# A four-stage attention and FFN kernel on Trainium2: the hidden units of the expert stage are split before they are transposed, and the order of four engines around it is rewritten

## What is computed

```python
router_logits = x2d @ gate_kernel                      # 2048 x 32
routing_weights, selected_experts = jax.lax.top_k(jax.nn.softmax(router_logits, axis=-1), 8)
routing_weights = routing_weights / jnp.sum(routing_weights, axis=-1, keepdims=True)
w0 = jax.lax.ragged_dot(sorted_inputs, gate_proj, group_sizes)    # 512 -> 192
w1 = jax.lax.ragged_dot(sorted_inputs, up_proj, group_sizes)      # 512 -> 192
inter = jax.nn.silu(w0) * w1
expert_out = jax.lax.ragged_dot(inter, down_proj, group_sizes)    # 192 -> 512
output = jnp.einsum('BKE,BK->BE', per_token, routing_weights)
```

## Time and profile before

| | |
|---|---|
| median of three runs | 1451.62 us |
| profiled execution, first to last instruction (span) | 1474.3 us |
| mean granted TensorE clock in it | 0.977 of full speed |
| PE busy, matmuls | 1382.7 us, 94% |
| DVE, ACT, POOL busy | 1022.1, 505.4, 383.7 us |
| expert stage, first hidden transposition to the last | 871.8 to 1461.9 us |

### The profile page before, as it was taken

The page is one execution under the profiler, slowest core; times in us unless marked ns, Lnnn a source line. Parts: engine busy times, 40 slices in busy tenths (PEclk is TensorE's granted clock), DMA queues, the critical chain, the costliest instruction groups (busy, mean ns, idle before and its releaser), DMA issues.

```text
span 1474.3 us, 26984 instructions
## 1 busy us (share of the span) xinstructions
PE 1382.7 (94%) x7525; PEld 753.2 (51%) x7526; DVE 1022.1 (69%) x2467; ACT 505.4 (34%) x916; POOL 383.7 (26%) x313
## 2 busy tenths in 40 slices
PE   4799999999999999999999559999999999999997
PEld 3344444444444444455444236666666666666664
DVE  7879857976895656688776536666666666666664
ACT  1454543444435343422222113333333333333332
POOL 1000000000000000025556543444344344344443
PEclk9899999999999999999999769999999999999999
DMA  9975776766767778836748668889999888989785
GB/s 370 396 262 193 263 256 213 247 197 205 241 209 237 235 254 286 280 119 251 284 195 294 242 227 216 223 218 260 246 246 234 221 229 228 247 223 222 148 162 84
DMA packets 132696, 345.04 MB, mean 234 GB/s; under 512 B 15008, under 2 KB 19616, under 8 KB 125728
## 3 DMA queue, kind: packets, MB, share of 16 engines
q1 hardware_dynamic: 73488, 206.72, 41.6%
q0 software_dynamic: 34640, 85.74, 25.2%
q10 hardware_dynamic: 24512, 51.89, 10.8%
HBM read 192.68 MB, written 151.62 MB: 234 GB/s over the span
## 4 chain that ended last, share of the span: by engine, by line
PE 68%; DVE 16%; DMA 4%; issue 4%; ACT 3%; another core or an unknown queue 2%; ACTq 1%; SPq 1%; DVEq 0%; POOLq 0%
PE PS L1671 17%; PE PS L1673 17%; PE PS L1672 17%; PE PS L1933 5%; PE PS L1961 2%; PE PS L1962 2%; DMA split_experts<-HT 2%; DMA CST<-in_kv 1%; PE PS L1950 1%; DVE EX L1300 1%; PE PS L1951 1%; DVE EX L1306 1%; DVE nw L1027 1%; DMA X<-in_x 1%
## 5 line engine op out<-in xcount | busy, mean ns | idle before, releaser
L587 POOL DMA_INDIRECT out<-BIG,EX x159 | 247.2, 1555 | 354.9 <-issue 153.4
L1671 PE MATMUL PS<-BIG 128*128 (+1 forms) x795 | 269.5, 339 | 5.0 <-DVE BIG L1572 3.3
L1672 PE MATMUL PS<-BIG 128*128 (+1 forms) x795 | 269.5, 339 | 0.0
L1673 PE MATMUL PS<-BIG 128*128 (+1 forms) x795 | 269.5, 339 | 0.0
L1671 PE MATMUL PS<-HT,BIG 128*128 128x512 f16 (+1 forms) x512 | 194.1, 379 | 3.0 <-DVE HT L1101 1.4
L1672 PE MATMUL PS<-HT,BIG 128*128 128x512 f16 (+1 forms) x512 | 194.0, 379 | 0.0
L1673 PE MATMUL PS<-HT,BIG 128*128 128x512 f16 (+1 forms) x512 | 194.0, 379 | 0.0
L560 POOL DMA_INDIRECT rows_by_expert<-HT,POS x128 | 124.9, 976 | 122.6 <-DVE POS L1391 88.1
L1672 PE MATMUL PS<-BIG,EX 128*128 128x512 f16 (+1 forms) x376 | 143.8, 382 | 1.1 <-issue 1.1
L824 ACT ACTIVATE BIG<-PS 128x256 f16<-128x256 f32 x159 | 61.1, 384 | 243.3 <-PE PS L1951 229.0
L1673 PE MATMUL PS<-BIG,EX 128*128 128x512 f16 (+1 forms) x376 | 143.6, 382 | 0.4 <-issue 0.4
(11 more groups left out here) (264 smaller groups left out, 2218.0 us busy)
## 6 DMA issues: line engine op xcount, KB each, us to landing
BIG<-rows_by_expert ACTq DMA_DIRECT2D x159, 280.0 KB
HT<-in_experts SPq DMA_DIRECT2D x64, 640.0 KB, 4.6
BIG<-split_experts SPq DMA_DIRECT2D x32, 1152.0 KB
split_experts<-HT SPq DMA_DIRECT2D x96, 320.0 KB, 2.2
CST<-in_kv SPq DMA_DIRECT2D x64, 256.0 KB, 4.7
split_context<-RT SPq DMA_DIRECT2D x64, 256.0 KB, 4.5
BIG<-split_context SPq DMA_DIRECT2D x7, 2048.0 KB
rows_by_expert<-X SPq DMA_DIRECT2D x32, 280.0 KB
```

The costliest lines, as they stand in the source:

```text
L587: pool.indirect_dma_start(a_out, bass.IndirectOffsetOnAxis(ap=IDY[:, u % V:u % V + 1], axis=0), yt[u % V], None, compute_op=ALU.add).then_ ...
L1671: mm(out, lh, rh, start=first, stop=False)
L1672: mm(out, lh, rl, start=False, stop=False)
L1673: return mm(out, ll, rh, start=False, stop=last_group)
```

## The change

- **Hidden units.** They are split where they lie, by tokens: ACT rounds to fp16 (`hidden_hi`, 192 columns), DVE subtracts (`hidden_lo`, two pieces of 64 and 128 columns). The four pieces are laid in a row: high 0 to 127, high 128 to 191 beside low 128 to 191, low 0 to 127. PE transposes these three 128 by 128 blocks in fp16 into a PSUM tile of fp16, and ACT copies the 384 columns to SBUF (`hidden_copy`).
- **Down weights.** The second block of 64 rows is now stacked high over high and low over low, so `tile_down` still has five matmuls; an expert takes 2 EW = 5120 columns, 1280 KB, and `split_half` is two equal instructions on DVE in place of three.
- **Order.** In pass t PE runs: transposition of t+3, up of t+2, hidden transposition of t+1, down of t. ACT, DVE follow; LEAD is 7.
- **Registers.** In the loop ACT loads 8 rows and 12 due counts in place of 12 and 16; the counts go through a maximum (`load_counts`), on POOL too. `CH` is one element longer, so all tables lie four bytes further on.
- **First tiles.** ACT issues the gathers 1 to 3, then `tile_silu(0)`, `tile_hi(1)`, the gather of 4 and so on. Two tables that ACT needs first are made and announced first; a further small matmul (PS bank 6) serves them. POOL writes column 4 of token tile 13 ahead of tiles 14 and 15. SP stores the empty rows of eight experts before the loop, not of four.

```diff
-E16 = EW + EL
+E16 = 2 * EW
-LEAD = 6
+LEAD = 7
+LATE = 1
+def load_counts(eng, name, table, least, most):
+    loaded = [eng.alloc_register(f"{name}{i}") for i in range(table.shape[-1])]
+    held = [eng.alloc_register(f"{name}_held{i}") for i in range(table.shape[-1])]
+    eng.reg_load(loaded, table)
+    for to, of in zip(held, loaded):
+        eng.reg_alu(to, of, least, ALU.max)
...
-        CH = ex(1, F16)
+        CH = ex(2, F16)
...
-            for e in range(WP):
+            for e in range(2 * WP):
                 pad_expert(e, 16 * e)
...
-            for t in range(NT - 3, NT):
+            scatter_rows(NT - 3, range(5))
+            for t in range(NT - 2, NT):
                 scatter_rows(t, range(4))
...
             def hidden_hi(t, p):
-                act.wait_ge(s_at, t + 1)
-                act.activation(eah[p], PS[:, 4, 0:2 * P], ACT.Copy).then_inc(s_ah2, 1)
+                act.wait_ge(s_ea, t + 1)
+                act.activation(es[p][:, 0:M], ea[p], ACT.Copy).then_inc(s_ah2, 1)
+            def hidden_copy(t, p):
+                act.wait_ge(s_at, t + 1)
+                act.activation(eT[p], hT, ACT.Copy).then_inc(s_ac, 1)
...
-            for t in range(1, LEAD):
-                act.wait_ge(s_add[t], LANDED)
-                load_tile(t, 0, rows[t], due[t])
-            tile_hi(1, 1, due[1])
-            tile_silu(0, 0)
+            for t in range(1, 4):
+                load_early(t)
+            tile_silu(0, 0)
+            tile_hi(1, 1, due[1])
+            load_early(4)
+            hidden_hi(0, 0)
+            tile_hi(2, 0, due[2])
+            load_early(5)
+            tile_silu(1, 1)
+            hidden_copy(0, 0)
+            hidden_hi(1, 1)
+            load_early(6)
...
             def hidden_lo(t, p):
                 dve.wait_ge(s_ah2, t + 1)
-                v.tensor_tensor(eal[p], PS[:, 4, 0:2 * P], eah[p], ALU.subtract).then_inc(s_al2, 1)
+                v.tensor_tensor(es[p][:, M:2 * P], ea[p][:, P:M], es[p][:, P:M], ALU.subtract)
+                v.tensor_tensor(es[p][:, 2 * P:3 * P], ea[p][:, 0:P], es[p][:, 0:P], ALU.subtract).then_inc(s_al2, 1)
...
-            def hidden_transpose(p):
-                nc.tensor.transpose(PS[:, 4, 0:P], ea[p][:, 0:P], ident[:, :])
-                nc.tensor.transpose(PS[:, 4, P:2 * P], ea[p][:, P:2 * P], ident[:, :]).then_inc(s_at, 1)
+            def hidden_transpose(t, p):
+                if not isinstance(t, int) or t:
+                    pe.wait_ge(s_ac, t)
+                pe.wait_ge(s_al2, t + 1)
+                for k in range(3):
+                    last = nc.tensor.transpose(hT[:, k * P:(k + 1) * P], es[p][:, k * P:(k + 1) * P], ident16)
+                last.then_inc(s_at, 1)
...
-                    tile_transpose(t + 2, (u + 2) % U, it + (u + 2) // U)
-                    pe.wait_ge(s_ea, t + 1)
-                    hidden_transpose(u % 2)
-                    tile_up(t + 1, (u + 1) % 2, at[u + 1])
+                    tile_transpose(t + 3, (u + 3) % U, it + (u + 3) // U)
+                    tile_up(t + 2, u % 2, at[u + 2])
+                    hidden_transpose(t + 1, (u + 1) % 2)
                     tile_down(t, u % 2, at[u])
```

More of the change, by code:

```diff
@@ L263, in build @@
         o += 2 * M
[L264 to L267, removed]
+        ea = [BIG[:, o + i * M:o + (i + 1) * M] for i in range(2)]
+        o += 2 * M
+        es = [f16(BIG, o + i * M, (2 * M,)) for i in range(2)]
+        o += 2 * M
+        eT = [f16(BIG, o + i * 192, (3 * P,)) for i in range(2)]
         o = [0]
@@ L284, in build @@
         TODD = ex(TABLE, I32, p=1)
+        TROWS = TWK[:, 0, :].bitcast(I32)
         TPAD = ex(NE, I32, p=1)
@@ L844, in _ @@
             act.wait_ge(s_tab, 1)
-            rows, due = rows_at("first_row", 0, U), experts_due("first_due", 0, U)
+            first = [act.alloc_register(f"first{i}") for i in range(2 * U)]
+            act.reg_load(first[0:U], TROWS[0:1, 0:U])
+            act.reg_load(first[U:], TAB[0:1, 1, 0:U])
+            rows = [act.snap(x, donate=True, min_val=0, max_val=NE * CAP + (SPARES - 1) * P) for x in first[LATE:U]]
+            due = [act.alloc_register(f"first_due{i}") for i in range(U - LATE)]
@@ L863, in _ @@
+                    tile_silu(t + 2, u % 2)
+                    hidden_copy(t + 1, (u + 1) % 2)
+                    hidden_hi(t + 2, u % 2)
             t = LOOPS * U
-            rows, due = rows_at("last_row", t + LEAD, REST - LEAD), experts_due("last_due", t + 2, REST - 2)
+            due = experts_due("last_due", t + 3, REST - 3)
             for u in range(REST):
-                hidden_hi(t + u, u % 2)
+                if u + 3 < REST:
+                    tile_hi(t + u + 3, (u + 3) % 2, due[u])
@@ L867, in _ @@
                 if u + 2 < REST:
-                    tile_hi(t + u + 2, u % 2, due[u])
-                if u + LEAD < REST:
-                    load_tile((u + LEAD) % U, t + u + (V + LEAD - U + 1), rows[u], due[u + LEAD - 2])
+                    tile_silu(t + u + 2, u % 2)
                 if u + 1 < REST:
-                    tile_silu(t + u + 1, (u + 1) % 2)
+                    hidden_copy(t + u + 1, (u + 1) % 2)
+                if u + 2 < REST:
+                    hidden_hi(t + u + 2, u % 2)
@@ L1589, in _ @@
             tile_lo(0, 0)
+            hidden(0, 0)
             tile_lo(1, 1)
-            hidden(0, 0)
+            hidden_lo(0, 0)
+            tile_lo(2, 0)
+            hidden(1, 1)
+            hidden_lo(1, 1)
             with dve.Fori(0, LOOPS) as it:
```

161 lines of the change are left out of this document (84 added, 77 removed).

## The result

| | before | after |
|---|---|---|
| median | 1450.05 us (4 runs, 1448.45 to 1452.07) | **1504.44 us** (4 runs, 1496.59 to 1509.23) |
| ratio, 95% interval | | **1.0362** (1.0324 to 1.0400) |
| profiled execution, span | 1474.3 us | 1505.5 us |

The changed kernel is 54 us slower. The forecast was 1438.3 us, 1428 to 1449: sign and size are wrong. The ratios in this document leave out disturbed executions, 30 to 39 us longer than the others: three of the six of `c_align16`, its profiled one among them, and one each of `c_early`, `c_best` and `d_scatter`.

The account below looks back on a forecast made before the run. PE issuing without pause was taken as the bound (98.8% of the expert stage). Gains of 8.9 (transpositions), 1.5 (branches) and 2.9 us (hand-over) sum to 13.3, taking 1451.6 to 1438.3 us, range 1428 to 1449.

Parts of the forecast that it names:

- Branches: At loop branches, ACT reading 20 registers for 28 shortens PE's waits: 1.5 us gained, between 0 and 4.
- the paragraph on cover: In the expert stage, PE's 3.6 us of other work hides the new hidden-unit chain of 2.0 us and some hand-overs.
- The slack of 0.2 and of 0.75 us: At a bad loop branch, ACT's spare time before PE must wait, rising from about 0.2 to 0.75 us.
- Transpositions: In each PE pass, three fp16 hidden transpositions at 0.054 us replace two float32 ones: 8.9 us gained.
- The rival of 0.11 us each: On PE, an fp16 transposition costs as much as a float32 one: slower, 1464.7 us; chance 0.07.
- The estimate of 44 us: On PE, the third hidden transposition paid in full at 0.275 us for 159 tiles; the prediction did not adopt it.
- Cover of the hidden chain: Waiting for the new hidden-unit chain costs PE nothing, as 3.6 us of other PE work precedes its transposition.
- DMA: Loading 1280 for 1152 KB per expert, storing 128 KB more and extra empty rows cost nothing.
- the second rival: Pass stays at 3.69 us because DMA engines or POOL's adds become the limit: 1447.2 us, or 1451; chance 0.12.
- Hand-over: Between attention and expert stage: 1.6 us from ACT's new order plus 1.27 from one POOL scatter fewer, 2.9 us gained.
- the first rival: Moving ACT's gathers removes its wait between attention and expert stage: 9.6 us plus 3.0 of clock, 1428.6 us; chance 0.15.
- The one for slower: On PE, fp16 transpositions at 0.11 us each add 17.5 us, less 4.4: 1464.7 us; chance 0.07.

Follow-up runs that it names:

- c_align16: Changed kernel with three padding elements ahead of the tables, which then start 16 bytes on from a 32-byte boundary: 1432.3 us, 0.9871 of before.
- c_early: `a_align32` with all gathers of the first tiles (1 to 6) issued ahead of the first silu: 1440.33 us, 0.9930 of before.
- c_best: `a_align32` with eight registers instead of seven read behind the loop by PE, DVE and POOL: 1432.38 us, 0.9873 of before.
- d_scatter: `a_align32` with POOL's last scatters in the order of the kernel before: 1433.69 us, 0.9874 of before.
- the fourth: Extra fp16 transposition of 128 by 128 behind each tile's three, added to the changed kernel with tables on a 32-byte boundary: 1440.70 us, 0.9939 of before.
- a_align32: Changed kernel with tables moved on by seven more elements, to a multiple of 32 bytes: 1464.32 us, 0.9897 of before.
- b_counts: Kernel before with only the maxima on ACT's due counts and POOL's start places added: 1.0025 of before.
- d_counts: Same kernel as `b_counts`, run again on the other chip: 1.0014 of before.
- a_align8: Changed kernel with tables moved on by one more element, to a multiple of 8 bytes but not 16: 1530.19 us, 1.0349 of before.
- c_pe_off: `a_align32` with PE's loads alone made unaligned in the loop, one register and then eleven: 1473.93 us, 1.0171 of before.

## Why the prediction was wrong

**The step that failed is "Branches".** It counted registers, 20 for 28, and so expected shorter loads, 1.5 us of gain between 0 and 4. The duration of a load hung on where its table begins. The row that I used, 1.84 us at one branch, was an aligned load of 16 registers and an unusual one: in the same trace most loads of 12 take 0.79 to 0.84 us and most of 16 take 1.00 to 1.10. The tables' new start, which the section on the change states ("all tables lie four bytes further on"), was given no price at all, and so no bounds. In its place: ACT's loads take at least 1.77 for 0.56 us with 8 registers and 2.59 for 0.78 with 12, and those of PE, DVE and POOL rise alike; 67 us are lost in the stage. With loads of that length the paragraph on cover would have given the direction: 4.4 us of loads and 0.8 around them against 3.6.

The maxima, bounded by "nothing and 0.55 us" of slack, cost the order of before 2.0 to 3.7 us in all. Without slow loads the new order has next to no wait at branches (0.7 us from 900 to 1450), so there the new slack does what I said, and more: of the 4 us that I put there I took back 1.5, and all are gone. The slack of 0.2 and of 0.75 us in that paragraph cannot be worked out from its rows.

**Transpositions: right.** 0.056 us each by the fourth, a pass 3.684 to 3.633 us, 159 x 0.051 = 8.1 us for my 8.9. The rival of 0.11 us each fell. The estimate of 44 us, which pays the 275 ns of the Trainium skill's page (TensorE: Matmul & The Clock Gate, Part 4: PE-mode transpose) in full, fell with it.

**Cover of the hidden chain: right.** In `a_align32` PE waits 0.5 us once for it between 900 and 1450 us.

**DMA: right.** At a share of 0.98 PE is still full; the second rival fell.

**Hand-over: the size depends on the chip.** Where ACT has the unexplained wait, start against start gives 7.5 - 5.2 = 2.3 us, and the first rival is wrong there. That is more than the 1.6 that I gave to ACT's order; the other 1.27 of my 2.9, one scatter fewer, is not there. POOL writes as many scatters as before, and one of them now stands ahead of those that gathers 1 to 3 wait for: with the old order (`d_scatter`) up of tile 1 starts 3.3 us ahead of the last scatter, in `c_best` 1.6, and the times are the same. Where ACT has not that wait, the rival's mechanism is right, as ACT stood behind its gathers, but not its size: 3.7 us of start and some 2 of clock for its 9.6 and 3.0. I gave it 0.15 because the one trace had ACT standing after its last gather.

**The profile against the median.** I put the 22.7 us between them down to the recording. More likely it is a chip: on that of `a_align32` before takes 1479.3 us, on the other 1449.4, and recorded executions agree with their medians in both, within 4 us. The record does not name the chip of the first profile; its last scatter, at 864.84 us, fits the slower one, and the changed kernel's first hidden transposition, at 850.1, fits the faster, so the two spans in the table above are not to be compared. POOL's last scatter starts at 867.70 us in `b_counts` and at 844.87 in `d_counts`, the same kernel: the difference lies ahead of the expert stage. It did no harm to the sum.

**The sum.** With the slow loads taken out, 15.0 and 19.1 us were measured for my 13.3, on the two chips: 1432.4 us for 1438.3, inside the range. Part of that is luck: branches and hand-over gave more than I took, the scatter nothing. These are a few us; what turned the sign is 72 us from four bytes.

Nor did any rival cover it. The one for slower stood on PE's transpositions, while the trace already had register loads of 1.84 us on the path. Longer loads at all 19 branches would have been the right one, with the point from which it decides: 3.6 us of cover.

## What to carry to other kernels

When a table in SBUF that engines read into registers is moved, or an allocation ahead of it grows, look at where each load now begins: keep starts on 16 bytes, and pad if needed. Price the things that a change moves without saying so (addresses, offsets) like those that it says, and give the slower rival to the row that is already on the path. At a hand-over, put the instruction that PE waits for ahead of DMA issues that wait for others.

## What the runs showed of the hardware

- A register load from a 16-byte boundary in SBUF takes ACT 0.33 us for 4 registers, 0.56 for 8 and 0.78 for 12 (`a_align32`), 0.22 for four more; from 4 or 8 bytes off it, 1.77 for 8 and 2.59 to 2.62 for 12 (the changed kernel, `a_align8`), 0.21 for one more. PE's twelve rise from 0.85 to 2.87 us, DVE's eight from 0.60 to 1.85, POOL's eight from 0.57 to 1.84. These are the shortest ones of each kind; single loads of ACT take up to 1.8 times as long off the boundary (3.23 for 1.77 us, the changed kernel) and over twice as long on it (1.30 for 0.56 us, `a_align32`). The steps fit loads that go four registers at a time when aligned and one by one otherwise; that this is how they work is an inference.
- The Trainium skill gives about 200 ns a register, also in bulk, for register loads that it describes as loads from HBM (Runtime: NRT & Kernel Launch, Instruction fetch mechanics). The unaligned loads from SBUF here come to the same, 0.21 us a register; the aligned ones show 0.07.
- The Trainium skill also gives a floor of about 600 ns for such a load, against which the compiler unrolls by four (DMA: Bandwidth & Descriptors, Latency and other measured facts). The runs do not bear the floor out for SBUF: one register takes 0.31 us in `c_pe_off`, four aligned ones 0.33.
- An fp16 transposition of 128 by 128 costs PE 0.056 us in a row of others; one in float32 0.11.
- A pause of PE of 1.2 us left the clock at 1.00 (window 1046 to 1052 us of the changed kernel, below); one of 2.9 us was followed by starts twice as far apart.

```profile
1046.00:1052.00 6.00, 4.81 (x31) 2.75 (x30) 1.51 (x5) 1.12 (x4) 0.00 (x0) 1.00 0.81 176
```
